# Wide layer: the search's first level from half the columns, and levels and counts kept in pairs

## The reference

```
z = x_flat @ ternary_quant(W_syn).T + b_syn
k = max(1, int(N * (1.0 - TARGET_SPARSITY)))      # N = 1024, k = 102
topv, _ = jax.lax.top_k(z, k)
thresh = topv[:, -1:]
hidden = jnp.where(z >= thresh, jax.nn.relu(z), 0.0)
out = hidden @ ternary_quant(W_out).T + b_out
return layernorm(x + out, gamma, beta)
```

## Time and profile before

| | us |
|---|---|
| median of 3 runs | 1194.39 (1192.79 to 1199.39) |
| the profiled execution | 1195.06 |
| its span | 1193.3 |
| VectorE busy | 904.9 (76%) |
| TensorE busy | 1084.1 (91%) |
| ScalarE busy | 625.9 (52%) |
| the wide layer, from the first filler product to the last residual add | 447.6 to 690.1 |

### The profile page before, as it was taken

One profiled execution on the slowest core, in us unless ns is written; L12 is line 12 of the kernel. 1 busy time (PEld: TensorE's weight loads), 2 busy tenths in 40 slices (PEclk: granted clock), 3 DMA queues, 4 the chain that ended last, 5 costly groups with the idle time before them and its releaser, 6 DMA issues. The chain is left out here.

```text
span 1193.3 us, 18401 instructions
## 1 busy us (share of the span) xinstructions
PE 1084.1 (91%) x7046; PEld 745.7 (62%) x7046; DVE 904.9 (76%) x1698; ACT 625.9 (52%) x1096; POOL 216.0 (18%) x176
## 2 busy tenths in 40 slices
PE   8889999999999989777867889999997899999998
PEld 8623333333333437566757768888886698989976
DVE  7689999999999634689888886555553878798853
ACT  5338787887887764776641233333333433433343
POOL 1308100000000002000034203000000744554410
PEclk9879999999999999998987999999998999999999
DMA  5852033123120001000000020010101000000020
GB/s 198 235 133 55 17 40 54 24 34 55 31 26 2 2 1 32 1 1 1 11 9 1 1 93 33 21 36 19 36 1 50 14 1 1 1 1 1 1 67 5
DMA packets 25290, 40.02 MB, mean 34 GB/s; under 512 B 3560, under 2 KB 12784, under 8 KB 25200
## 3 DMA queue, kind: packets, MB, share of 16 engines
...
...
q10 hardware_dynamic: 576, 0.00, 0.0%
...
## 5 line engine op out<-in xcount | busy, mean ns | idle before, releaser
L771 DVE TENSOR_REDUCE att_mx<-att_ps_m 128x2 f32<-128x1024 f32 x256 | 310.9, 1224 | 23.6 <-PE att_ps_m L637 19.9
L748 ACT ACTIVATE att_prob<-att_ps_s 128x512 f32<-128x512 f32 x512 | 278.2, 596 | 88.5 <-PE att_ps_s L687 76.5
L703 PE MATMUL att_ps_o<-att_prob,v_rows 128*32 128x256 f32 (+1 forms) x1920 | 159.3, 405 | 0.0
L1980 POOL TENSOR_TENSOR qry_prod<-qry_qr,lin_ksum 128x512 f32<-128x512 f32 x64 | 92.9, 1451 | 303.7 <-ACT qry_qr L2102 289.6
L687 PE MATMUL att_ps_s<-qst,kst 50*128 50x512 f32 x512 | 128.0, 496 | 11.0 <-ACT att_prob L748 10.4
L687 PEld LDWEIGHTS att_ps_s<-qst,kst 50*128 50x128 f32 x512 | 48.0, 183 | 123.8 <-ACT att_prob L748 114.2
L637 PE MATMUL att_ps_m<-kst,qst 48*128 48x512 f32 x512 | 109.9, 424 | 8.8 <-DVE att_mx L771 7.2
L2102 ACT ACTIVATE qry_qr<-qry_ps_q 128x512 f32<-128x512 f32 x64 | 38.3, 598 | 132.8 <-PE qry_ps_q L153 124.0
L153 PE MATMUL qry_ps_o<-qry_m,qry_n_hi 128*128 128x256 f32 x512 | 99.5, 293 | 0.5 <-DVE qry_n_lo L2010 0.5
L703 PEld LDWEIGHTS att_ps_o<-att_prob,v_rows 128*32 128x32 f32 x1920 | 38.1, 108 | 84.7 <-ACT att_prob L748 71.1
L1692 DVE SCALAR_TENSOR_TENSOR key_k_lo<-kf_ps,key_k_hi 128x512 fp32r<-128x512 f32 x64 | 44.2, 691 | 61.6 <-ACT key_k_hi L1770 61.0
...
## 6 DMA issues: line engine op xcount, KB each, us to landing
...
```

The costliest lines, as they stand in the source:

```text
L703: ins = nc.tensor.matmul(ps_o[32 * h:32 * h + 32, cols], vall[:, NS * b + s, h0 + h, :], prob[:, u % PR, h, cols], start=s == 0, stop=s == ...
L748: nc.scalar.activation(prob[:, u % PR, 2 * j + r, :], ps_s[:, (n + r) % BANKS, :], ACT.Exp).then_inc(exp_ok, 1)
L771: nc.vector.reduce_max(mx[:, v % 2, :, m], ps_m[:, n % 2], AX.X).then_inc(m_rd, 1)
L1980: nc.gpsimd.tensor_tensor(prod[:, u % 2, :], qr[:, u % 2, :], ksum[:, b, cols(n)], ALU.mult).then_inc(pr_ok, 1)
```

## The change

The statistics of a row are taken from the first 512 of its 1024 columns. The level and the count of a chunk stand side by side in one tile (`now`), and so do the two ends with their counts (`ends`), so that one predicated copy moves a level with its count; both masks come from one instruction. ScalarE counts Sign(level - z), with the level as bias, and `nlev` is gone. The threshold is picked from nine values, the level and the eight largest, by one comparison. Fewer instructions are linked.

```diff
-        zst = st.sb("zst", [P, TPC, NH, 6])
+        zst = st.sb("zst", [P, TPC, 6])
...
-        lev = st.sb("lev", [P, d.NT])
-        nlev = st.sb("nlev", [P, d.NT])
+        now = st.sb("now", [P, d.NC, 2, TPC])
         sgn = st.sb("sgn", [P, d.NT])
-        cnt = st.sb("cnt", [P, d.NT])
-        lo, hi, clo, chi = (st.sb(n, [P, d.NT]) for n in ("lo", "hi", "clo", "chi"))
+        ends = st.sb("ends", [P, 2, 2, TPC])
+        width = st.sb("width", [P, 2, TPC])
+        below_end = st.sb("below_end", [P, 2, TPC])
+        msk = st.sb("msk", [P, 2, TPC])
+        doubt = st.sb("doubt", [P, 2 * TPC])
...
-        top = st.sb("top", [P, d.NT, 8])
+        top = st.sb("top", [P, d.NT, 9])
+        place = st.sb("place", [P, 9])
...
+                link(nc.gpsimd.memset(below_end[:, 0, :], 1.0))
+                link(nc.gpsimd.memset(below_end[:, 1, :], 0.0))
...
@@ -1022,103 +1026,94 @@
                 def spread(t):
 
                     dve.wait_ge(ring_rd, nth("z", t))
-                    for n in range(NH):
-                        ins = nc.vector.bn_stats(zst[:, t % TPC, n, :], z_tile(t)[:, n * d.CH:(n + 1) * d.CH])
-                    return ins
+                    return nc.vector.bn_stats(zst[:, t % TPC, :], z_tile(t)[:, 0:d.CH])
 
                 def spreads(c):
                     for j in range(TPC):
-                        ins = nc.vector.bn_aggr(zmv[:, j, :], zst[:, j].rearrange("p a b -> p (a b)"))
+                        ins = nc.vector.bn_aggr(zmv[:, j, :], zst[:, j])
                     ins.then_inc(zvar, 1)
                     dve.wait_ge(zvar, c + 1)
 
                 def first_level(c):
                     cs = slice(TPC * c, TPC * (c + 1))
                     dve.wait_ge(zroot, c + 1)
-                    link(nc.vector.scalar_tensor_tensor(out=lev[:, cs], in0=zsd[:, cs], scalar=SPREAD0,
-                                                        in1=zmv[:, :, 0], op0=ALU.mult, op1=ALU.add))
-                    nc.vector.tensor_scalar(nlev[:, cs], lev[:, cs], -1.0, None, ALU.mult).then_inc(lev_ok, 1)
-                    nc.vector.scalar_tensor_tensor(out=lo[:, cs], in0=zsd[:, cs], scalar=-0.6, in1=lev[:, cs],
-                                                   op0=ALU.mult, op1=ALU.add)
-                    nc.vector.scalar_tensor_tensor(out=hi[:, cs], in0=zsd[:, cs], scalar=0.6, in1=lev[:, cs],
-                                                   op0=ALU.mult, op1=ALU.add)
-                    nc.vector.memset(clo[:, cs], 122.0)
-                    link(nc.vector.memset(chi[:, cs], -68.0))
+                    nc.vector.scalar_tensor_tensor(out=now[:, c, 0, :], in0=zsd[:, cs], scalar=SPREAD0,
+                                                   in1=zmv[:, :, 0], op0=ALU.mult, op1=ALU.add).then_inc(lev_ok, 1)
+                    for side, (off, count) in enumerate(((-0.6, 122.0), (0.6, -68.0))):
+                        nc.vector.scalar_tensor_tensor(out=ends[:, side, 0, :], in0=zsd[:, cs], scalar=SPREAD0 + off,
+                                                       in1=zmv[:, :, 0], op0=ALU.mult, op1=ALU.add)
+                        ins = nc.vector.memset(ends[:, side, 1, :], count)
+                    link(ins)
 
                 def next_level(c, r):
 
                     cs = slice(TPC * c, TPC * (c + 1))
-                    LEV, CNT = lev[:, cs], cnt[:, cs]
+                    LEV, CNT = now[:, c, 0, :], now[:, c, 1, :]
                     dve.wait_ge(cnt_ok, TPC * (ROUNDS * c + r + 1))
-                    link(nc.vector.tensor_scalar(CNT, sgn[:, cs], 0.5, d.N / 2 - AIM, ALU.mult, ALU.add))
-
-                    link(nc.vector.tensor_tensor(t1[:], CNT, CNT, ALU.mult))
-                    link(nc.vector.tensor_scalar(missed[:, cs], t1[:], 16.5, None, ALU.is_gt))
+                    link(nc.vector.tensor_scalar(CNT, sgn[:, cs], -0.5, d.N / 2 - AIM, ALU.mult, ALU.add))
+                    square = nc.vector.tensor_tensor(t2[:], CNT, CNT, ALU.mult)
                     if r == ROUNDS - 1:
+                        link(square)
+                        link(nc.vector.tensor_scalar(missed[:, cs], t2[:], 16.5, None, ALU.is_gt))
                         return
-                    m = msk[:].bitcast(U32)
-                    link(nc.vector.tensor_scalar(msk[:], CNT, 0.0, None, ALU.is_gt))
-                    nc.vector.copy_predicated(lo[:, cs], m, LEV)
-                    link(nc.vector.copy_predicated(clo[:, cs], m, CNT))
-                    link(nc.vector.tensor_scalar(msk[:], CNT, 0.0, None, ALU.is_le))
-                    nc.vector.copy_predicated(hi[:, cs], m, LEV)
-                    link(nc.vector.copy_predicated(chi[:, cs], m, CNT))
+
+                    both = [P, 2, TPC]
+                    link(nc.vector.scalar_tensor_tensor(out=msk[:], in0=CNT.unsqueeze(1).to_broadcast(both), scalar=0.0,
+                                                        in1=below_end[:], op0=ALU.is_gt, op1=ALU.is_equal))
+                    nc.vector.tensor_scalar(missed[:, cs], t2[:], 16.5, None, ALU.is_gt)
+                    for side in range(2):
+                        ins = nc.vector.copy_predicated(ends[:, side],
+                                                        msk[:, side].bitcast(U32).unsqueeze(1).to_broadcast(both),
+                                                        now[:, c])
                     if r == 0:
                         link(nc.vector.scalar_tensor_tensor(out=t1[:], in0=CNT, scalar=1.0 / SLOPE, in1=zsd[:, cs],
                                                             op0=ALU.mult, op1=ALU.mult))
                         link(nc.vector.tensor_tensor(t1[:], t1[:], LEV, ALU.add))
                     else:
-                        nc.vector.tensor_tensor(t1[:], clo[:, cs], chi[:, cs], ALU.subtract)
-                        link(nc.vector.tensor_tensor(t2[:], hi[:, cs], lo[:, cs], ALU.subtract))
-                        nc.vector.reciprocal(t3[:], t1[:])
-                        link(nc.vector.tensor_tensor(t2[:], t2[:], clo[:, cs], ALU.mult))
+                        link(ins)
+                        link(nc.vector.tensor_tensor(width[:], ends[:, 0], ends[:, 1], ALU.subtract))
+                        nc.vector.reciprocal(t3[:], width[:, 1, :])
+                        link(nc.vector.tensor_tensor(t2[:], width[:, 0, :], ends[:, 0, 1, :], ALU.mult))
                         link(nc.vector.tensor_tensor(t2[:], t2[:], t3[:], ALU.mult))
-                        link(nc.vector.tensor_tensor(t1[:], t2[:], lo[:, cs], ALU.add))
-                    link(nc.vector.copy_predicated(LEV, missed[:, cs].bitcast(U32), t1[:]))
-                    nc.vector.tensor_scalar(nlev[:, cs], LEV, -1.0, None, ALU.mult).then_inc(lev_ok, 1)
+                        link(nc.vector.tensor_tensor(t1[:], ends[:, 0, 0, :], t2[:], ALU.subtract))
+                    nc.vector.copy_predicated(LEV, missed[:, cs].bitcast(U32), t1[:]).then_inc(lev_ok, 1)
 
                 def eight(c, js):
 
                     for j in js:
                         t = TPC * c + j
                         ins = nc.vector.scalar_tensor_tensor(out=below[:, t % 2, :], in0=z_tile(t),
-                                                             scalar=lev[:, t:t + 1], in1=z_tile(t),
+                                                             scalar=now[:, c, 0, j:j + 1], in1=z_tile(t),
                                                              op0=ALU.is_le, op1=ALU.mult)
                     link(ins)
                     for j in js:
                         t = TPC * c + j
-                        ins = nc.vector.max(top[:, t, :], below[:, t % 2, :])
+                        ins = nc.vector.max(top[:, t, 1:9], below[:, t % 2, :])
                     link(ins)
 
                 def threshold(c):
 
                     cs = slice(TPC * c, TPC * (c + 1))
-                    LEV, THR = lev[:, cs], thr[:, cs]
-
-                    link(nc.vector.tensor_scalar(t1[:], cnt[:, cs], -1.0, KEEP - 1 - AIM, ALU.mult, ALU.add))
-                    nc.vector.tensor_scalar(t2[:], t1[:], -1.0, None, ALU.is_equal)
-                    link(nc.vector.tensor_tensor(pick[:], t1[:].unsqueeze(2).to_broadcast([P, TPC, 8]),
-                                                 iota8[:].unsqueeze(1).to_broadcast([P, TPC, 8]), ALU.is_equal))
-                    nc.vector.tensor_tensor(t2[:], t2[:], LEV, ALU.mult)
+                    LEV, CNT, THR = now[:, c, 0, :], now[:, c, 1, :], thr[:, cs]
+
+                    nc.vector.scalar_tensor_tensor(out=doubt[:, 0:TPC], in0=LEV, scalar=0.0, in1=missed[:, cs],
+                                                   op0=ALU.is_le, op1=ALU.max)
+                    link(nc.vector.tensor_tensor(doubt[:, TPC:], top[:, cs, 1], LEV, ALU.is_equal))
+                    nc.vector.reduce_max(flag[:, 0:1], doubt[:], AX.X).then_inc(flag_ok, 1)
+                    nc.vector.tensor_copy(top[:, cs, 0], LEV)
```

(43 more changed lines are left out.)

2 lines of the change are left out of this document (1 added, 1 removed).

## The result

The changed kernel takes 1182.52 us (median of 6 runs, 1181.58 to 1189.13), the kernel before 1195.8 on the same chip (6 runs): ratio 0.9897, 95% interval 0.9879 to 0.9916, so 13.3 us faster by the medians and 12.3 (10.0 to 14.5) by the ratio. Of these 5.6 us 2.7 lie in the layer and 2.9 behind it. The other stages scatter too: those before the layer took 451.07 us in after and 447.58 in before, those behind it 504.81 and 503.23, and over all the traces here they vary by 4.3 and 3.9 us. So the layer is read by itself.

The account below looks back on a forecast made before the run. The prediction took the wide layer as a relay between VectorE and ScalarE, no engine full. Its walked gains summed to 13.0 us, from 1195.06 to 1182.0 profiled, forecast median 1181.4 us, range 1177.5 to 1187.

Parts of the forecast that it names:

- Rounds, first level, threshold in a quiet place: VectorE's search: round 0 takes 1.20 us, rounds 1 and 2 1.78, first level gains 0.20, threshold takes some 1.1.
- Step 5: Layer step of VectorE and ScalarE alone, no new rows entering: rounds 0, 1, 2 of chunk 3 gain 3.03 us.
- Threshold of chunk 3: Step 6, beside GpSimd: 5.9 us becomes 2.5, through before the long GpSimd instruction; gain 3.4, bounds 0.86 and 4.8.
- Rival (a): Threshold of chunk 3 still meets the long GpSimd instruction, gaining 0.9 and not 3.4: 1183.9 us; chance 0.14.
- the walk: Step-by-step sum along the wide layer's path of the savings that reach its end: 13.0 us.
- Step 3: Round 0 of chunk 1 gains 1.0, round 1 0.75 on ScalarE, slack before VectorE waits for the projection 2.06.
- Steps 1 and 2: Chunk 0's statistics, aggregation and level gain 0.85; its round 0 gains 1.03; chunk 1's first level 0.20.
- Step 4: TensorE's step, its products following one another: VectorE's savings end in waits, gain 0.
- the first level and the cast: Walked between step 3's slack and step 4: quicker first level and one linked cast less gain 0.35 us.
- rival (b): TensorE's clock returns to 2.4 GHz sooner in step 4, gaining about 2.4 us more: 1179.0 us; chance 0.14.
- Rival (d): ScalarE and TensorE set every step, so little arrives; gain up to 5 us: 1190; chance 0.07.
- Rival (e): One missed row of 2048 sends its chunk through the general routine, 122 us: about 1303 us; chance 0.03.

Follow-up runs that it names:

- all_linked: The changed kernel with every instruction of the rounds and the threshold linked to the next, their number unchanged: 1189.0 us, ratio 0.9938 to the kernel before.
- again: The changed kernel run once more with nothing changed, for a second profiled execution: 1183.52 us, ratio 0.9892 to the kernel before.
- old_threshold: The changed kernel with the earlier threshold set back (12 instructions, 8 linked): 1186.43 us, ratio 0.9913 to the kernel before.
- the kernels with filler: fill_all compared with before_fitted, the changed kernel and the kernel before, both with longer TensorE filler: 1175.72 and 1191.89 us.
- fill_all: The changed kernel with filler products on TensorE lengthened where its trace shows it idle, three behind step 4's turn: 1175.72 us, ratio 0.9824 to the kernel before.
- fill_seven: fill_all with seven filler products, not three, behind the turn of step 4: 1175.08 us, ratio 0.9823 to the kernel before.
- before_fitted: The kernel before with TensorE filler lengthened to fit its own gaps: 1191.89 us, ratio 0.9961 to the kernel before.

## Why the prediction was right, and where it was not

**Rounds, first level, threshold in a quiet place**: 1.20, 1.78 and 1.1 forecast, 1.18, 1.77 and 1.09 measured. The two constants of the earlier trace rows, 0.20 linked and 0.08 free, carry to runs not yet seen; `all_linked` shows that both parts, fewer instructions and fewer links, are real: its round 0 with nine linked instructions takes 1.68 us, between 2.23 and 1.18.

**Step 5** (3.03 forecast): 2.99 in after, 2.99 in again. VectorE and ScalarE alternate there, so each tenth arrives.

**Threshold of chunk 3** (3.4): 3.87 on the instructions themselves, and 3.29 by `old_threshold`. Rival (a) did not come. From the end of step 5 to the end of the layer the walk had 3.77; the kernels with filler show 3.74, after only 2.33. Term missing: the new gap of TensorE in step 7, which costs 1.4, and the 0.45 by which L115 now meets GpSimd.

**Step 3** (3.81): 5.6. This is the step of the walk that failed in size. The forecast let VectorE run into the projection with the duration read in before, 5.41 us for 16 products, and gave the rest up to that wait. The wait is there, but those 5.41 were products partly in a dip; in after they took 3.72, 1.69 less. TensorE of before, then of after, in these stretches (the clock is the last but two):

```profile
530.01:535.42 5.41, 5.41 (x19) 4.49 (x19) 4.74 (x30) 2.72 (x5) 0.00 (x0) 0.68 0.00 0
```

```profile
532.15:535.87 3.72, 3.72 (x19) 3.31 (x19) 2.85 (x15) 3.33 (x6) 0.00 (x0) 1.00 0.00 0
```

A row shown once was taken for the price of the instruction, where the earlier trace rows had the price at full clock. With 3.72 in its place the walk gives 5.5 for this step and leaves VectorE 0.8 us of waiting where it had 2; VectorE of after:

```profile
535.98 1.22 DVE L1004 TENSOR_TENSOR residual<-residual,mlp_ps_t 128x1024 f32<-128x1024 f32 x1 [0.77 <-PE mlp_ps_t L1369]
```

It is 0.80 in again. `all_linked`, whose projection took 5.41, has the other case: a wait of 1.55 and a gain of 2.97. With the right price the statistics reach the end with about 2 us, not 0.7.

**Steps 1 and 2** (2.08): 1.50 gained in again, 0.63 lost in after. Between the kernels with filler it is 2.74; less the 0.65 by which the products of step 1 happen to start sooner in `fill_all` this is 2.09, and 0.86 and 1.88 at the two events before (0.85 and 1.88 forecast). The arithmetic was right; what the walk had no term for is TensorE's clock, whose dips in steps 1 and 2 fall on products that the layer waits for.

**Step 4** (0, and 0.35 for the first level and the cast): 0.65 in after, 0.94 in again. The 0.35 did not arrive: where the flag is read, VectorE's idle time grew from 1.24 to 1.59 us, in after, in again and in `fill_all`; why is open. What arrived is rival (b) in part: turn and filler together take 0.6 and 0.9 us less than in before, and the step is shorter by almost just that, as the clock came back sooner. (b) had up to 2.4; with filler, TensorE does save 2.3 there (`fill_seven`), but VectorE is then last, and the step is 1.9 shorter than in before. The 2.66 of the last column has 0.76 in it from the dip in `before_fitted`.

**The total** is right within 0.3 us by the medians and 0.7 by the ratio, and that is in part luck, because errors cancel: 1.8 too little in step 3 and 0.3 to 0.6 in step 4, against 0.6 to 2.7 missing in steps 1 and 2 and 1.1 to 1.4 behind step 5. The layer gained 2.0 less than walked in after, and 0.7 more in again. Rival (d) is out by the layer's 11 to 13.7 us. Rival (e) did not come: no instruction of the general routine runs in after. Its price was 142, not 122. Beyond step 1, which of the dips costs how much in one execution was not settled; their places change from one execution to the next.
